# One step deeper projection pipeline, an early query projection, and ScalarE's square root in a six-layer windowed attention kernel

## The chip, the core and the metric

The kernel runs on one core of a Trainium2 chip. The metric is the device time of one execution in microseconds; several executions are timed, and one more is profiled.

## What is computed

The input is one sequence of 2048 tokens with 128 channels. First comes a recurrent mixing layer (RWKV-like) with its normalisation, which the change does not touch. Then come six layers, each of windowed attention and a gated feed-forward block, and a last normalisation. Per layer, cut to what matters here:

```
x = attn(shift_tokens(x)) + x          # half of the channels are taken from the token before
x = ffn(shift_tokens(x)) + x
attn:  q, k, v = split(x @ Wqkv)       # 16 heads of 64
       q = l2norm(q) * q_scale         # t / max(norm(t), 1e-12)
       k = l2norm(k) * k_scale
       q = q*cos*scale + rotate_half(q)*sin*scale;   k likewise with 1/scale
       window of 32: each query sees its own block and the block before it
       softmax(8 * q @ k.T + mask) @ v, then @ Wo
ffn:   layernorm -> @ W1 + b1 -> a * gelu(gate) -> @ W2 + b2
```

## The kernel before

The program is written by hand in raw instructions: each engine has its own queue of instructions, and semaphores with counts order them (`after(engine, semaphore, n)` waits for a count of n, and for nothing where n is not positive). Tokens are cut into 16 tiles of 128 (`TILES`), so six layers have 96 tile steps, numbered through the layers (`STEPS`, `tile_of`, `layer_of`). Activations lie channel by token in `xa` (before attention) and `xb` (after it).

`layers()` is a software pipeline. Each engine's `step(s, h, odd, live)` does, for step s, the parts of several tiles in one fixed order:

- **p = s+1**, projection: TensorE projects q (L1278) into `proj_a`, k (L1293) into `proj_b`, and later v (L1350) into `proj_a`. ScalarE squares q and k (L1054), VectorE sums the squares per head (L1155), takes the inverse root of the sums by nine small operations (`inverse_root`, L88 to L104: a guess from the exponent's bits, two polishing steps), and scales q and k to `unit` (L1180). The rotation is `across` (GpSimd, L999), `along` (GpSimd for q at L1032, VectorE for k at L1233) and their sum `rotated` (GpSimd, L1006). ScalarE copies v to `val` (`v_tok`, L1114).
- **a = s**, scores: TensorE transposes q and k (L1246, to `turn`), ScalarE copies them out (L1083, L1089), TensorE adds the mask (L1332) and makes the scores (L1338), VectorE takes the row maxima and subtracts them (L1169, L1172), ScalarE takes the exponential (L1061).
- **b = s-1**, output: TensorE transposes the probabilities (L1246), ScalarE copies them (L1074), TensorE mixes the values (L1312, semaphore `mixed`), VectorE divides by the mass (L1161), TensorE transposes the heads (L1246) and multiplies by Wo (L1379), VectorE adds to `xb` (L1223).
- Every second step has one part of the feed-forward block of a pair of tiles. **Odd** steps have `down`: Gelu on ScalarE (L1068), the gating on VectorE (L1196, semaphore `gated`), W2 on TensorE (L1357), the sum into `xa` (L1219); and the deviations of the next pair (L1363, L1131, L1132). **Even** steps have `up`: the normalised tile is transposed (L1372), scaled (L1122), and multiplied by W1 at the end of TensorE's step (`widen`, L1262).

TensorE's order in a step is: transposes of the probabilities (b), query projection (p), key projection (p), transposes of q (a), the mix (b), transposes of k (a), transposes of the heads (b), mask and scores (a), value projection (p), down and deviations or the normalised tile's transposes, Wo (b), and in even steps the wide projection. The key projection waits in odd steps for `gated` (L1285), since the wide projection's output leaves the same bank. The query projection waits for `v_laid` of the tile before (L1275), that is for ScalarE's copy of v out of the bank.

**The values' way.** The mix needs v by windows of 64 keys (the own block of 32 and the one before) on the right partitions. So after each copy of v, SyncE issues 16 transfers of 64 KB from `val` to `v_win` (`spread`, L933 to L948). `val` and `v_win` have two buffers each. The counts that order this are:

```
spread(m):   wait v_laid >= m + 1;  wait mixed >= 2 * (m - 1)     # L936, L938; mixed counts 2 per tile
             16 transfers, each adds 16 to v_spread               # 256 per spread
ScalarE's copy of v of tile p:   wait v_projected >= 2 * p + 2;  wait v_spread >= 256 * p     # L1112, L1113
TensorE's mix of tile b:         wait v_spread >= 256 * b + 256                               # L1306
```

SyncE's queue also holds the weight loads of the next layer, each behind the last use of the old ones, between the spreads.

The steps before s = 7 and the last ones are written out (`run`, L919), the 88 between them are a loop of 44 rounds of an odd and an even step on every engine.

Of the kernel before, what the change touches and what calls it, by code (L numbers as in the profile page):

```python
# [25 lines left out]
I32 = mybir.dt.int32  # L26
# [36 lines left out]
ROOT_SCALE = 3 / 8  # L63
# [15 lines left out]
ROOT_OPS = 9  # L79


def inverse_root(dve, ops, x, bound, y, work, magic, done, before):

    for i in ops:
        if i:
            dve.wait_ge(done, before + i)
        if i == 0:
            op = dve.scalar_tensor_tensor(bound, x, 1e-24, x, ALU.max, ALU.max)  # L88
        elif i == 1:
            op = dve.scalar_tensor_tensor(y.bitcast(I32), bound.bitcast(I32), -0.5, magic.bitcast(I32), ALU.mult, ALU.add)  # L90
        elif i == 2:
            op = dve.tensor_tensor(work[0], y, y, ALU.mult)
        elif i == 3:
            op = dve.tensor_tensor(work[1], work[0], bound, ALU.mult)
        elif i == 4:
            op = dve.scalar_tensor_tensor(work[0], work[1], -10.0 / 3.0, work[1], ALU.add, ALU.mult)
        elif i == 5:
            op = dve.scalar_tensor_tensor(y, work[0], 5.0, y, ALU.add, ALU.mult)
        elif i == 6:
            op = dve.scalar_tensor_tensor(work[0], y, -0.5 * ROOT_SCALE ** 2, y, ALU.mult, ALU.mult)  # L100
        elif i == 7:
            op = dve.tensor_tensor(work[1], work[0], bound, ALU.mult)
        else:
            op = dve.scalar_tensor_tensor(y, work[1], 1.5, y, ALU.add, ALU.mult)  # L104
        op.then_inc(done, 1)
# [711 lines left out]
def layers(nc, ctx, given):  # L817
# [12 lines left out]
    with ExitStack() as own:  # L830
# [8 lines left out]
        magic = sb("magic", [128, 2, HEADS])  # L839
# [4 lines left out]
        sums_min = sb("sums_min", [128, 2, HEADS])  # L844
# [5 lines left out]
        rotated = [sb(f"rotated{i}", [128, HEADS, HEAD]) for i in range(2)]  # L850
# [21 lines left out]
        warm = sb("warm", [128, 1])  # L872

        warmed = sem("warmed")
# [7 lines left out]
        rooted = sem("rooted")  # L882
# [19 lines left out]
        FIRST, ROUNDS = 7, 44  # L902
# [27 lines left out]
        with nc.Block() as block:  # L930
            @block.sync
            def _(sp):
# [23 lines left out]
                for m in range(5):  # L956
                    spread(m, m % 2)
                with sp.Fori(0, 5) as i:
                    spread(i * 2 + 5, 1)
                    spread(i * 2 + 6, 0)  # L960
                with sp.Fori(1, DEPTH) as layer:
# [12 lines left out]
                    load_when(load_down, xa_ready, layer * (TILES // 2) + XA_BASE, layer)  # L974
                    with sp.Fori(0, 5) as i:
                        spread(first + i * 2 + 5, 1)
                        spread(first + i * 2 + 6, 0)
                spread(STEPS - 1, 1)

            @block.gpsimd  # L980
            def _(pool):
# [19 lines left out]
                def add_turned(j, p):  # L1001
# [546 lines left out]
```

## Time and profile before

| | |
|---|---|
| median of 3 runs | 2007.84 us (2001.0 to 2007.87) |
| the profiled execution | 2001.63 us, span in the trace 1999.8 us |
| TensorE matmuls busy | 1771.6 us (89% of the span) |
| VectorE busy | 1543.1 us (77%) |
| GpSimd busy | 1454.8 us (73%) |
| ScalarE busy | 1156.1 us (58%) |
| granted TensorE clock, mean | 0.975 |
| first and last query projection of a step (L1278) | 194.6 and 1922.6 us |

In the rows, PE is TensorE's matmuls, PEld its weight loads, DVE VectorE, ACT ScalarE, POOL GpSimd, SP SyncE and SPq its queue. L12 is line 12 of the kernel. A helper's line stands for all its calls: L1246 is every transpose. Times are in microseconds from the start of the span, durations of one are in ns where the view says so. A matmul's end is modelled: a row's length reaches somewhat beyond the start of the next group, so distances between starts tell more. "PEclk" is the granted clock as a share of full speed.

### The profile page before, as it was taken

The numbers are of one execution on the slowest core, as the hardware profiler recorded it, in microseconds if no ns is written. First come the engines' busy times: TensorE is split into PE (matmuls) and PEld (weight loads), VectorE is DVE, ScalarE is ACT, GpSimd is POOL, SyncE is SP. The second block draws the span as 40 slices with busy tenths as digits, with TensorE's granted clock in tenths as the row PEclk, the third lists the DMA queues.
The fourth block names the chain that finished last, engine by engine and source line by source line (L and its number), as shares of the span: only waits on it lengthen the run. The fifth ranks groups of instructions, "written<-read, shape, count | busy, mean of one in ns | idle before, by whom it ended". The sixth has DMA issues, their size and how long they took to land. (4 is left out here: it accounts for less than half of the span.)

```text
span 1999.8 us, 85355 instructions
## 1 busy us (share of the span) xinstructions
PE 1771.6 (89%) x34184; PEld 1277.4 (64%) x34184; DVE 1543.1 (77%) x2729; ACT 1156.1 (58%) x1966; POOL 1454.8 (73%) x967
## 2 busy tenths in 40 slices
PE   7764789999999999999999999999999999999995
PEld 3453466666666666666666666666666666666664
DVE  4774798778878877788788777887887788778864
ACT  2311456666666666666666666666666666666663
POOL 3221787787788778877887787778777877887771
PEclk9985899999999999999999999999999999999998
DMA  4000222223232223222223322233222232322220
GB/s 151 2 3 1 56 63 57 64 60 84 66 74 58 54 55 94 63 68 58 63 56 85 76 67 55 52 81 81 62 58 62 61 86 63 74 60 52 55 63 22
DMA packets 93581, 123.43 MB, mean 62 GB/s; under 512 B 27760, under 2 KB 41808, under 8 KB 93392
## 3 DMA queue, kind: packets, MB, share of 16 engines
q1 hardware_dynamic: 93232, 122.42, 24.3%
q8 instruction: 46, 0.75, 0.2%
q10 hardware_dynamic: 288, 0.13, 0.0%
q14 instruction: 15, 0.12, 0.0%
HBM read 20.74 MB, written 1.05 MB: 11 GB/s over the span
## 5 line engine op out<-in xcount | busy, mean ns | idle before, releaser
L999 POOL TENSOR_TENSOR across<-unit,turns 128x1024 f32<-128x1024 f32 x192 | 497.4, 2591 | 275.5 <-issue 265.6
L1006 POOL TENSOR_TENSOR rotated<-along,across 128x1024 f32<-128x1024 f32 x192 | 495.7, 2582 | 14.2
L1155 DVE TENSOR_REDUCE sums<-squares 128x16 f32<-128x1024 f32 x192 | 234.0, 1219 | 177.9 <-ACT squares L1054 177.7
L1246 PE MATMUL turn<-identity,rotated 128*128 128x128 f32 x1536 | 204.7, 276 | 35.5 <-POOL rotated L1006 34.3
L1246 PEld LDWEIGHTS turn<-identity,rotated 128*128 128x128 f32 x1536 | 172.3, 141 | 98.0 <-issue 82.5
L1032 POOL TENSOR_TENSOR along<-unit,turns 128x1024 f32<-128x1024 f32 x96 | 228.0, 2375 | 0.0
L1350 PE MATMUL proj_a<-w_qkv,shift_a 128*128 128x512 f32 x384 | 189.5, 616 | 36.3 <-DVE unit L1180 30.1
L1114 ACT COPY val<-proj_a 128x1024 f32<-128x1024 f32 x96 | 97.2, 1012 | 180.7 <-PE proj_a L1350 180.7
L1379 PE MATMUL att<-o_t,w_o 128*128 128x128 f32 x1536 | 188.9, 277 | 0.0
L1278 PE MATMUL proj_a<-w_qkv,shift_a 128*128 128x512 f32 x384 | 184.4, 603 | 5.0 <-POOL shift_a L989 3.7
L1379 PEld LDWEIGHTS att<-o_t,w_o 128*128 128x128 f32 x1536 | 181.0, 193 | 1.0 <-issue 1.0
L1089 ACT COPY k_t<-turn 128x512 f32<-128x512 f32 x192 | 103.2, 589 | 134.5 <-PE turn L1246 134.5
L1293 PE MATMUL proj_b<-w_qkv,shift_a 128*128 128x512 f32 x384 | 180.9, 593 | 0.0
L1233 DVE TENSOR_TENSOR along<-unit,turns 128x1024 f32<-128x1024 f32 x96 | 165.7, 1726 | 0.0
L1054 ACT ACTIVATE squares<-proj_a 128x1024 f32<-128x1024 f32 x96 | 98.2, 1023 | 115.8 <-PE proj_a L1278 115.8
L1312 PE MATMUL att<-v_win,p_t 64*32 64x64 f32 x12288 | 154.2, 225 | 0.8 <-ACT p_t L1074 0.8
L1338 PEld LDWEIGHTS turn<-k_t,q_t 64*32 64x32 f32 x12288 | 128.3, 105 | 41.4 <-issue 41.1
L1074 ACT COPY p_t<-att 128x512 f32<-128x512 f32 x192 | 103.1, 589 | 89.0 <-PE att L1246 89.0
L1312 PEld LDWEIGHTS att<-v_win,p_t 64*32 64x32 f32 x12288 | 135.6, 105 | 20.1 <-issue 16.9
L1161 DVE TENSOR_TENSOR heads_out<-att,inv_mass 128x512 f32<-128x512 f32 x192 | 123.6, 686 | 31.4 <-PE att L1312 31.4
L1338 PE MATMUL turn<-k_t,q_t 64*32 64x64 f32 x12288 | 144.2, 225 | 0.0
L1172 DVE TENSOR_TENSOR logits<-turn,row_max 128x512 f32<-128x512 f32 x192 | 132.8, 692 | 6.7
(201 smaller groups left out, 3366.2 us busy)
## 6 DMA issues: line engine op xcount, KB each, us to landing
v_win<-val SPq DMA_DIRECT2D x1536, 64.0 KB, 2.0
w_qkv<-wqkv_dram SPq DMA_DIRECT2D x18, 512.0 KB, 3.9
w_o<-wo_dram SPq DMA_DIRECT2D x6, 512.0 KB, 4.7
where<-positions_dram SPq DMA_DIRECT2D x1, 2048.0 KB, 10.7
w_ffn<-ffn_dram SPq DMA_DIRECT2D x12, 170.5 KB, 2.3
w_ffn<-ffn_dram SPq DMA_DIRECT2D x6, 192.0 KB, 2.3
x_tok<-x_dram SPq DMA_DIRECT2D x4, 256.0 KB, 4.2
out_dram<-final SPq DMA_DIRECT2D x4, 256.0 KB, 2.4
```

Of the source, the lines that this page charges most:

```text
L999: pool.tensor_tensor(a[:, :, ::-1, :], u, table, ALU.mult).then_inc(acrossed[j], 1)
L1006: pool.tensor_tensor(rotated[j][:, :, :], along[j][:, :, :], across[j][:, :, :], ALU.add).then_inc(rotated_in[j], 1)
L1032: pool.tensor_tensor(along[0][:, :, :], unit[0][:, :, :], turns[mine][:, 0, :].unsqueeze(1).broadcast_to([128, HEADS, HEAD]), ALU.mult).th ...
L1155: dve.tensor_reduce(sums[:, j, :], squares[j][:, :, :], AX.X, ALU.add).then_inc(summed[j], 1)
L1233: dve.tensor_tensor(along[1][:, :, :], unit[1][:, :, :], turns[mine][:, 2, :].unsqueeze(1).broadcast_to([128, HEADS, HEAD]), ALU.mult).the ...
L1246: mm = pe.transpose(bank[:, TILE * (i % 4):TILE * (i % 4) + TILE], buffer[:, TILE * i:TILE * i + TILE], identity[:, :])
L1278: mm = pe.matmul(bank_a[:, half, :], shift_a[mine][:, :], w_qkv[:, 512 * half:512 * half + 512], start=True, stop=True)
L1293: mm = pe.matmul(bank_b[:, half, :], shift_a[mine][:, :], w_qkv[:, base:base + 512], start=True, stop=True)
L1312: mm = pe.matmul(bank_s[WINDOW * w:WINDOW * w + WINDOW, par, HEAD * a_:HEAD * a_ + HEAD], p_t[rows, a_, WINDOW * w:WINDOW * w + WINDOW], v ...
L1338: mm = pe.matmul(bank_t[WINDOW * w:WINDOW * w + WINDOW, par, HEAD * a_:HEAD * a_ + HEAD], q_t[rows, a_, WINDOW * w:WINDOW * w + WINDOW], k ...
L1350: pe.matmul(bank_a[:, par, :].rearrange("p (a e) -> p a e", a=PAIRS), shift_a[mine][:, :], values[:, par, :, :], start=True, stop=True).th ...
L1379: mm = pe.matmul(bank_s[:, 0, 0:TILE], w_o[:, a_, :], o_t[:, a_, :], start=(a_ == 0), stop=(a_ == PAIRS - 1))
```

## The change

- **Depth.** The projection part works on p = s+2 instead of s+1, on every engine. So `rotated` gets two buffers by the parity of the tile, and a tile's q and k are transposed two steps after their projection. The pipeline starts at s = -2; the loop has 43 rounds, and the parities of `turns`, `shift_a` and `val` are turned.
- **Early query projection.** The query projection of tile s+3 is issued at the end of step s, after Wo and before the wide projection. Its squares are the first thing in ScalarE's next step, ahead of the Gelus and the copies of the probabilities; their sum is the first thing in VectorE's, ahead of the mass.
- **Root.** ScalarE takes a Relu with bias -1e-24 and a Sqrt with bias 1e-24 of the 128x32 sums, between the copies of q and of k. VectorE takes the reciprocal and one Newton step, four operations instead of nine, behind a wait for ScalarE's root. The factor 3/8 in the position tables goes with the old root.
- **Sets of functions.** ScalarE loads the set of sqrt ahead of the k squares and the set of exp behind the carry of the keys, in each step; the warming exponential of odd steps (L1093) goes.
- **SyncE.** The order of spreads and weight loads is shifted by one spread at four places. `spread` itself, and the two waits of the copy of v, are as they were.

The diff, cut to its core (the parity renamings, `mine` to `odd` for p, are left out):

```diff
-ROOT_OPS = 9
+ROOT_OPS = 4
+TINY = 1e-24
...
+def inverse_root(dve, x, root, y, work, done, before):
+
+    dve.reciprocal(y, root).then_inc(done, 1)
+    dve.wait_ge(done, before + 1)
+    dve.scalar_tensor_tensor(work[0], y, -0.5, y, ALU.mult, ALU.mult).then_inc(done, 1)
+    dve.wait_ge(done, before + 2)
+    dve.scalar_tensor_tensor(work[1], x, TINY, work[0], ALU.max, ALU.mult).then_inc(done, 1)
+    dve.wait_ge(done, before + 3)
+    dve.scalar_tensor_tensor(y, work[1], 1.5, y, ALU.add, ALU.mult).then_inc(done, 1)
...
-        rotated = [sb(f"rotated{i}", [128, HEADS, HEAD]) for i in range(2)]
+        rotated = [[sb(f"rotated{i}_{k}", [128, HEADS, HEAD]) for i in range(2)] for k in range(2)]
...
-        FIRST, ROUNDS = 7, 44
+        FIRST, ROUNDS = 7, 43
...
-            return {"p": 0 <= s + 1 < STEPS, "a": 0 <= s < STEPS, "b": 0 <= s - 1 < STEPS, "next": 0 <= s + 2 < STEPS,
+            return {"p": 0 <= s + 2 < STEPS, "a": 0 <= s < STEPS, "b": 0 <= s - 1 < STEPS, "next": 0 <= s + 3 < STEPS,
...
-            for s in range(-1, FIRST):
+            for s in range(-2, FIRST):
...
                     load_when(load_projection, k_projected, first, layer, 1)
+                    spread(first - 2, 0)
                     load_when(load_projection, v_projected, 2 * first, layer, 2)
                     spread(first - 1, 1)
                     spread(first, 0)
+                    spread(first + 1, 1)
                     load_when(load_wo, attended, first, layer)
-                    spread(first + 1, 1)
                     spread(first + 2, 0)
+                    spread(first + 3, 1)
                     load_when(load_up, widened, layer * (NC_ * TILES // 2), layer)
-                    spread(first + 3, 1)
                     spread(first + 4, 0)
                     load_when(load_down, xa_ready, layer * (TILES // 2) + XA_BASE, layer)
...
-                    after(pool, (q_turned, k_turned)[j], 2 * p)
+                    after(pool, (q_turned, k_turned)[j], 2 * (p - 1))
...
             def _(act):
...
-                    p, a, b, mine = s + 1, s, s - 1, 1 - odd
+                    p, a, b, mine = s + 2, s, s - 1, 1 - odd
...
+                    if live["p"]:
+                        square(0)
                     if live["down"]:
...
                     if live["p"]:
-                        square(0)
+                        act.preload_act_table_set("sqrt_and_others")
                         square(1)
...
+                    if live["p"]:
+                        act.wait_ge(summed[0], p + 1)
+                        act.wait_ge(summed[1], p + 1)
+                        after(act, rooted, ROOT_OPS * p)
+                        act.activation(lifted[:, :, :], sums[:, :, :], ACT.Relu, bias=tiny[:, 0:1]).then_inc(above_tiny, 1)
+                        act.wait_ge(above_tiny, p + 1)
+                        act.activation(root[:, :, :], lifted[:, :, :], ACT.Sqrt, bias=tiny[:, 1:2]).then_inc(roots_in, 1)
...
-                    if live["down"]:
-                        after(act, warmed, h)
-                        act.activation(warm[:, :], ones[:, 0:1], ACT.Exp).then_inc(warmed, 1)
...
+                        act.preload_act_table_set("exp_and_others")
                     if live["p"]:
                         act.wait_ge(v_projected, 2 * p + 2)
                         after(act, v_spread, 256 * p)
...
             def _(dve):
...
+                    if live["p"]:
+                        sum_squares(0)
                     if live["b"]:
                         dve.wait_ge(weighed, 2 * b + 2)
...
                     if live["p"]:
-                        sum_squares(0)
                         sum_squares(1)
...
+                        dve.wait_ge(roots_in, p + 1)
+                        inverse_root(dve, sums[:, :, :], root[:, :, :], inv_norm[:, :, :],
+                                     [w[:, :, :] for w in root_work], rooted, ROOT_OPS * p)
...
             def _(pe):
...
+                def project_queries(m, parity):
+                    pe.wait_ge(shifted, 2 * m + 2)
+                    pe.wait_ge(q_in, (layer_of(m) + 1) * 16)
+                    after(pe, v_laid, m)
+                    stand_alone(pe, passed)
+                    for half in range(2):
+                        mm = pe.matmul(bank_a[:, half, :], shift_a[parity][:, :], w_qkv[:, 512 * half:512 * half + 512],
+                                       start=True, stop=True)
+                    mm.then_inc(q_projected, 1)
...
                         mm.then_inc(attended, 1)
+                    if live["next"]:
+                        project_queries(s + 3, mine)
                     if live["up"]:
                         pe.wait_ge(normed_f, h + 2)
...
+                project_queries(0, 0)
                 run(pe, step)
```

## Rows read from the trace of the kernel before

**Rows 1.** one stretch: us; busy PE, PEld, DVE, ACT, POOL, PEclk, DMA share
```profile
663.80:1027.60 363.80, 338.44 (x6597) 246.60 (x6596) 292.63 (x509) 230.22 (x389) 291.83 (x190) 1.00 0.26 65
```

**Rows 2.** the waits, waiting line, releaser: us in all, times, longest us
```profile
PE turn L1246 <- POOL rotated L1006: 34.3, 51, 1.9
```

**Rows 3.** time line of TensorE: start us, us, what, [idle before <-releaser]
```profile
1002.45 1.96 PE L1350 MATMUL proj_a<-w_qkv,shift_a 128*128 128x512 f32 x4 [0.49 <-DVE unit L1180]
...
1008.56 1.06 PE L1246 MATMUL att<-identity,probs 128*128 128x128 f32 x8 [0.62 <-issue]
1009.46 1.88 PE L1278 MATMUL proj_a<-w_qkv,shift_a 128*128 128x512 f32 x4
1011.18 1.88 PE L1293 MATMUL proj_b<-w_qkv,shift_a 128*128 128x512 f32 x4
1012.89 1.04 PE L1246 MATMUL turn<-identity,rotated 128*128 128x128 f32 x8
1013.86 1.59 PE L1312 MATMUL att<-v_win,p_t 64*32 64x64 f32 x128
...
1020.28 1.96 PE L1350 MATMUL proj_a<-w_qkv,shift_a 128*128 128x512 f32 x4 [0.23 <-DVE unit L1180]
...
1024.40 1.99 PE L1262 MATMUL proj_b<-normed,w_ffn 128*128 128x256 f32 x8 [0.16 <-ACT normed L1122]
...
1027.10 1.04 PE L1246 MATMUL att<-identity,probs 128*128 128x128 f32 x8
```

**Rows 4.** time line of SyncE's queue, the first and last of one spread's sixteen
```profile
1005.78 0.51 SPq L945 DMA_DIRECT2D v_win<-val  x1
...
1015.21 0.59 SPq L948 DMA_DIRECT2D v_win<-val  x1
```

**Rows 5.** DMA issues on the page: count, KB each, us from issue to landing
```profile
v_win<-val SPq DMA_DIRECT2D x1536, 64.0 KB, 2.0
```

**Rows 6.** time line of ScalarE around two value copies
```profile
1004.52 1.01 ACT L1114 COPY val<-proj_a 128x1024 f32<-128x1024 f32 x1 [1.99 <-PE proj_a L1350]
...
1022.35 1.01 ACT L1114 COPY val<-proj_a 128x1024 f32<-128x1024 f32 x1 [1.73 <-PE proj_a L1350]
...
1024.88 1.28 ACT L1068 ACT_TABLE_LOAD   x1
1026.18 0.84 ACT L1068 ACTIVATE gelu<-proj_b,w_ffn 128x256 f32<-128x256 f32 x2
1027.30 0.47 ACT L1068 ACTIVATE gelu<-turn,w_ffn 85x256 f32<-85x256 f32 x1 [0.28 <-PE turn L1262]
```

**Rows 7.** groups by line and form: count, busy us, mean ns, idle before
```profile
L1155 DVE TENSOR_REDUCE sums<-squares 128x16 f32<-128x1024 f32 x192 | 234.0, 1219 | 177.9 <-ACT squares L1054 177.7
...
L1054 ACT ACTIVATE squares<-proj_a 128x1024 f32<-128x1024 f32 x96 | 98.2, 1023 | 115.8 <-PE proj_a L1278 115.8
...
L104 DVE SCALAR_TENSOR_TENSOR inv_norm<-root_work,inv_norm 128x32 f32<-128x32 f32 x96 | 18.4, 192 | 3.3
```

**Rows 8.** time line of VectorE, from the mass to the last gating
```profile
1026.00 1.21 DVE L1187 TENSOR_REDUCE mass<-probs 128x16 f32<-128x1024 f32 x1
...
1028.25 0.47 DVE L1196 SCALAR_TENSOR_TENSOR hidden<-turn,w_ffn,gelu 85x256 f32<-85x256 f32 x1
```

**Rows 9.** time line of TensorE, near the start and in the last steps
```profile
227.43 1.06 PE L1246 MATMUL att<-identity,probs 128*128 128x128 f32 x8 [2.53 <-ACT probs L1061]
...
1945.44 1.55 PE L1246 MATMUL turn<-identity,rotated 128*128 128x128 f32 x8 [1.95 <-POOL rotated L1006]
1946.78 1.91 PE L1246 MATMUL att<-identity,heads_out 128*128 128x128 f32 x8
1948.49 1.02 PE L1332 MATMUL turn<-band_bf,identity_bf 128*128 128x512 bf16 x2
```

**Rows 10.** time line of TensorE, the first two query projections
```profile
194.66 3.75 PE L1278 MATMUL proj_a<-w_qkv,shift_a 128*128 128x512 f32 x4 [3.68 <-POOL shift_a L989]
...
210.97 3.75 PE L1278 MATMUL proj_a<-w_qkv,shift_a 128*128 128x512 f32 x4 [1.30 <-ACT val L1114]
```

More of the change, by code:

```diff
@@ L955, in _ @@
                 sp.wait_ge(cleared, 2)
-                for m in range(5):
+                for m in range(6):
                     spread(m, m % 2)
-                with sp.Fori(0, 5) as i:
-                    spread(i * 2 + 5, 1)
+                with sp.Fori(0, 4) as i:
                     spread(i * 2 + 6, 0)
+                    spread(i * 2 + 7, 1)
                 with sp.Fori(1, DEPTH) as layer:
@@ L1011, in step @@
                 def step(s, h, odd, live):
-                    p, mine = s + 1, 1 - odd
+                    p = s + 2
                     if live["p"]:
@@ L1016, in step @@
                         after(pool, alonged[0], p - 1)
-                        pool.tensor_tensor(turns[mine][:, :, :], where[:, tile_of(p), :, :], scales[:, layer_of(p), :, :],
+                        pool.tensor_tensor(turns[odd][:, :, :], where[:, tile_of(p), :, :], scales[:, layer_of(p), :, :],
                                            ALU.mult).then_inc(table_made, 1)
@@ L1113, in step @@
                         after(act, v_spread, 256 * p)
-                        act.copy(v_tok[mine][:, :, :, :], bank_a[:, :, :].rearrange("p a (h e) -> p a h e", e=HEAD))\
+                        act.copy(v_tok[odd][:, :, :, :], bank_a[:, :, :].rearrange("p a (h e) -> p a h e", e=HEAD))\
                             .then_inc(v_laid, 1)
@@ L1149, in step @@
                 def step(s, h, odd, live):
-                    p, a, b, mine = s + 1, s, s - 1, 1 - odd
+                    p, a, b, mine = s + 2, s, s - 1, 1 - odd
                     def sum_squares(j):
@@ L1233, in step @@
                         dve.tensor_tensor(along[1][:, :, :], unit[1][:, :, :],
-                                          turns[mine][:, 2, :].unsqueeze(1).broadcast_to([128, HEADS, HEAD]),
+                                          turns[odd][:, 2, :].unsqueeze(1).broadcast_to([128, HEADS, HEAD]),
                                           ALU.mult).then_inc(alonged[1], 1)
@@ L1272, in step @@
                     if live["p"]:
+                        pe.wait_ge(k_in, (layer_of(p) + 1) * 16)
                         pe.wait_ge(shifted, 2 * p + 2)
-                        pe.wait_ge(q_in, (layer_of(p) + 1) * 16)
-                        after(pe, v_laid, p)
-                        stand_alone(pe, passed)
-                        for half in range(2):
-                            mm = pe.matmul(bank_a[:, half, :], shift_a[mine][:, :], w_qkv[:, 512 * half:512 * half + 512],
-                                           start=True, stop=True)
-                        mm.then_inc(q_projected, 1)
-                    if live["p"]:
-                        pe.wait_ge(k_in, (layer_of(p) + 1) * 16)
                         after(pe, united[1], p)
@@ L1292, in step @@
                             base = INNER + 512 * half
-                            mm = pe.matmul(bank_b[:, half, :], shift_a[mine][:, :], w_qkv[:, base:base + 512],
+                            mm = pe.matmul(bank_b[:, half, :], shift_a[odd][:, :], w_qkv[:, base:base + 512],
                                            start=True, stop=True)
@@ L1320, in step @@
                             pe.wait_ge(q_laid, 2 * a + j + 1)
[L1321 removed]
+                            transposes(bank_t[:, j, :], rotated_flat[odd][1], j, k_turned)
                     if live["b"]:
```

80 lines of the change are left out of this document (28 added, 52 removed).

## The prediction

> **What bounds the kernel now.** I read the busy time by stretch first, then the waits, and then one pair of steps in the order of time, because the change is made inside a loop whose body is such a pair. In the middle of the layers TensorE is busy 338 of 364 us, no other engine over 293, at a granted clock of 1.00, the full one of its two levels (2.4 GHz) [rows 1]. The first and the last query projection are 1728 us apart (194.6 to 1922.6) for 95 steps, 18.19 us a step, so that the stretch of 363.8 us is ten pairs of steps and a pair takes **36.38 us**. So TensorE's own work is nearly the bound, and what a better order can win is its waits. Two of them are what the deeper pipeline is aimed at: the transposes of q and k wait 34.3 us in all for GpSimd's sum [rows 2], and the value projection waits 0.49 and 0.23 us in a pair for the normalised heads [rows 3]. The time line shows two more, 0.62 us before the transposes of the probabilities after an odd step and 0.16 us before the wide projection [rows 3]. Together some 2 us of a pair: if all went and nothing came, 46.5 pairs would give 93 us back.
>
> I call a step odd where s is odd (it has the Gelu, the gating and the down projection) and even where the wide projection ends it. M is the end of a step's `mixed` matmuls (L1312).
>
> **The wait that decides.** The change leaves three conditions as they are and moves the work around them. ScalarE's copy of the values (L1114) waits for `v_spread` of 256*p, that is for all spreads up to p-1; with p = s+2 these are the spreads up to s+1, where before they were those up to s. SyncE's spread of m waits for the mix of m-2 (L938), so spread s+1 waits for the mix of s-1, and that is the one made **in the same step s**. Before, the spread that the copy needs began right after the copy of the step before (the row of SyncE at 1005.78 stands 0.25 us behind the end of the copy that starts at 1004.52) and issued its last transfer at 1015.21, 2.0 us before it landed [rows 4 to 6]: 1017.2, while the next copy started at 1022.35. It had 5.1 us to spare. Now it can't start before M = 1015.45 (1013.86 + 1.59 [rows 3]), so the spread would land at 1027.1 and the copy is 4.8 us late, 6.5 once the query projection no longer stands ahead of the value projection. Behind the copy on ScalarE's queue stand both exponentials and the normed copy; on TensorE the early query projection waits for `v_laid`, and everything of the next step stands behind it. That closes a ring from mix to mix.
>
> **The ring, piece by piece.** From M to the spread's first issue I take 0.25 us, the distance just read; fifteen distances of 0.629 us (1005.78 to 1015.21) are 9.43, the landing 2.0 [rows 4, 5]: 11.7. What a DMA's landing takes to release ScalarE no row shows; between 0 and the 0.25 of the other wake-ups I take 0.1. The copy therefore starts at M + 11.8. It lasts 1.01 [rows 6], TensorE wakes 0.25 later and the query projection takes 1.72 from start to start of the next (1009.46 to 1011.18) [rows 3]: the next group starts 2.98 us after the copy's start. The exponential and the normed copy that the wide projection needs are through by then (in the trace of before a Gelu load can start 2.53 us after the copy's start, with both exponentials done [rows 6]).
> - From an odd step into an even one there follow the transposes of the probabilities (0.90), the key projection (1.71), the transposes of q (0.97) and the mix (1.59) [rows 3]. Sum: 11.8 + 2.98 + 5.17 = **19.95 us**.
> - From an even step into an odd one the wide projection comes first (2.70), the probabilities' transposes end at 2.98 + 2.70 + 0.90 = 6.58 after the copy's start, and there the key projection waits for `gated`, because the gated values leave its bank. Before, the query projection stood between and covered this. The new order also puts the squares and the sum of q ahead of it: queries are ready at 1.26 + 1.88 = 3.14, the squares take 1.02, the set load for Gelu 1.28, three Gelus 1.6 with a wait inside, 1.3 without it (1026.18 to 1027.77) [rows 3, 6, 7], to about 6.9. On VectorE the sum of the q squares (1.22) runs from 4.3 to 5.5, and mass, reciprocal and three gatings take 2.72 (1026.00 to 1028.72) [rows 8]: 8.25. The key projection starts at 8.5, 1.9 late, the mix ends 4.27 later: 12.77. Sum: 11.8 + 12.77 = **24.55 us**.
>
> The pair takes 44.5 us instead of 36.38, so 8.1 more. The ring turns in steps 1 to 93, 46.5 pairs: **+377 us**.
>
> **The other parts.** *Root.* Nine small operations of VectorE become four behind two of ScalarE; five fewer at 0.19 us [rows 7] are some 1 us less on VectorE's queue, and a longer chain through a second engine; from the sum of the k squares to the value projection there are several us in the new schedule (TensorE has no work left from about M + 9 or 11 to M + 13), so I price both at nothing. If the ring were not there, this would be worth the 0.3 us a step that the value projection waits now [rows 3]. *Set loads.* The load of the exp set that the warming operation brings once in a pair goes and four come, five loads in a pair instead of two, 3.84 us of ScalarE at 1.28 each. The sqrt load stands ahead of the k squares, which come behind M; the exp load stands where ScalarE then waits for the spread. Priced at nothing, covered by the ring's 11.8; without the ring the sqrt load would delay the q copies by about 1 us a step. A Gelu starts 0.02 us after its load's end [rows 6], so a load costs its own row. The Trainium skill ("ScalarE: Activation LUTs", What ACT_TABLE_LOAD costs) counts a drain of about 1380 ns on top of the load's own 1283 at each switch to another set. By that rule the Gelus of each pair would come 1.38 us later behind the new squares, and the estimate from the page would be up to 64 us more than mine; no trace of before shows such a drain.
> *Early query projection.* The same four matmuls, elsewhere; counted in the ring. *GpSimd.* Its sum has a whole further step before it is read, so the 34.3 us of [rows 2] go, into a ring that is longer anyway. *SyncE.* The weight loads stay between the same spreads or move by one; a spread's transfers may queue behind one projection's load once or twice in each of five layers. Nothing to a few us each; I take nothing.
> *Start and end.* There is one more step that only projects: 16.3 us (194.66 to 210.97) [rows 10]. One full step of 18.2 goes and one without projections comes, 18.2 less three projections of about 1.8, 12.9. Net +11, I take **+10 us**.
>
> **The clock.** In the new schedule TensorE idles before each query projection: from the value projection (M + 7) the rest of an even step is about 2.3 us of work, an odd one's 3.7 (1020.28 to 1024.40, and 1002.45 to 0.62 before 1008.56, each less 1.8 for the value projection itself) [rows 3], so 3.9 us of idleness in an even step and some 2 in an odd one, and 1.9 more at the key projection. After an idle time of 1.95 us in the last steps two groups of eight transposes took 1.55 and 1.91 us instead of 1.04 [rows 3, 9], and the band's matmuls behind them 1.02: the clock was at its lower level (1.2 GHz), which cost 1.4 us in these two groups and, as I estimate, 1.7 with the band's. After 2.53 us near the start it did not fall (1.06) [rows 9]. So between nothing and both rings paying 1.7 to 2 (4 us a pair). I take one spell of 1.7 in each pair, since the one after 3.9 us is near certain but half absorbed by the 1.9 us that TensorE waits for `gated`, and the other comes about half of the time: **+79 us**.
>
> **Sum.** The profiled execution took 2001.63 us (span 1999.8), 0.3% under the median of the three runs, 2007.84, and near their lowest. 2001.6 + 377 + 79 + 10 = **2468 us**, 23% above it.
>
> **Rivals.**
> 1. *The copy does not wait, and the pipeline does what it is for.* It decides where the spread lasts less than the way from the mix to the end of the value projection, 1020.28 + 1.96 - 1015.45 = 6.8 us [rows 3], or where I misread the counts. Then a pair loses the 2.0 us of waits and gets the `gated` wait of 1.9, or not: 2001.6 + 10 and between 0 and -93, 1920 to 2010, middle 1960. For it: the waits of [rows 2] are real. Against it: sixteen issues at 0.629 us, and nothing in the change shortens them. 7 in 100, of which 4 below 1998.
> 2. *The clock falls in both rings of each pair and stays down longer* (6 us after short gaps that follow each other): 5 us a pair instead of 1.7, 2001.6 + 377 + 10 + 233 = 2620. For it: gaps in every step. Against it: 75% of busy time. 10 in 100.
> 3. *The ring holds, but the clock does not fall and the key projection does not wait*: 42.6 a pair, 2001.6 + 289 + 10 = 2300. 8 in 100.
> 4. *Slower by another wait alone*, the `gated` chain with the k squares behind the sqrt load, with no spread on the ring: 1.9 + 1 less the 2.0, 2001.6 + 42 + 10 = 2054. 3 in 100.
>
> **How the numbers follow.** The forecast has the remaining 72 in 100. Its own bounds: without a fall of the clock 2389, with 4 us a pair 2575; 0.1 us more or less at the landing moves it by 9. From 2340 to 2590 lie the forecast and the nearer halves of rivals 2 and 3; rivals 1 and 4 and the farther halves, 19 in 100, are left outside. 0.5% (10 us) is about what a measurement of this kernel can tell from no change. Faster than that: 4 in 100 (most of rival 1); within it: 2; slower: 94.
>
> **What would show it.** In the profile after: in each step the first transfer to v_win starts about 0.25 us behind the end of the mix instead of behind the value copy; ScalarE's idle time before the value copy grows from 1.7 us [rows 6] to more than 4, and ends with the transfers; the query projection starts 0.25 us after each copy; odd and even steps of 20 and 24.5 us; an idle 1.9 us before the key projection in odd steps; TensorE's busy share near 76% (36.4 less 2.0 of waits, in 44.5) and a clock below 1.00 in the middle stretches. The q transposes no longer wait for GpSimd. The prediction is wrong if the value copy follows its projection by less than 2 us, or if the spread's transfers come quicker when they start later; its size is wrong if a pair without falls of the clock is not near 44.5 us.

## The result, and the profile after

The changed kernel takes **2480.7 us** (median of 4 runs, 2474.4 to 2486.5) against 2005.7 us for the kernel before in the same rounds: ratio 1.237, 95% interval 1.233 to 1.241. The forecast was 2468 us. The profiled execution took 2482.8 us (span 2481.0).

The page, first part and clock; busy us (share) of each engine:

```profile
PE 1940.1 (78%) x34184; PEld 1354.8 (55%) x34184; DVE 1493.3 (60%) x2250; ACT 1373.1 (55%) x2253; POOL 1449.1 (58%) x965
...
PEclk9967888899999999999999999999999999999998
...
L1109 ACT COPY val<-proj_a 128x1024 f32<-128x1024 f32 x96 | 97.2, 1012 | 484.1 <-DMA v_win<-val 471.0
```

The stretch of [rows 1], now (us; busy PE, PEld, DVE, ACT, POOL; PEclk, DMA share, GB/s):

```profile
663.80:1027.60 363.80, 292.23 (x5167) 206.41 (x5155) 223.57 (x325) 216.36 (x355) 228.87 (x150) 0.94 0.22 53
```

The waits (total, times, longest):

```profile
ACT val L1109 <- DMA v_win<-val: 471.0, 93, 7.7
PE proj_a L1259 <- issue: 277.7, 86, 5.0
...
PE proj_b L1293 <- DVE hidden L1194: 62.9, 45, 1.8
```

Every engine is busy for a smaller share of the stretch than in [rows 1], so no engine became the bound: something makes them all wait. The waits name it. ScalarE's copy of the values waits for the spread's transfers 93 times, 5.1 us each. TensorE's query projection waits for that copy: the view puts 9 of its waits (37.3 us) down to it and 86 to "issue", but in the turn below the projections at 1210.36, 1231.55 and 1256.88 each start 0.10 us behind the end of a copy. The wait of [rows 2], for GpSimd's sum, has gone.

One turn of the ring. TensorE, from before a query projection in an odd step to the one after the next step:

```profile
1205.83 1.95 PE L1379 MATMUL att<-o_t,w_o 128*128 128x128 f32 x16
1210.36 2.44 PE L1259 MATMUL proj_a<-w_qkv,shift_a 128*128 128x512 f32 x4 [2.58 <-issue]
1212.60 1.91 PE L1244 MATMUL att<-identity,probs 128*128 128x128 f32 x8
1214.31 2.28 PE L1293 MATMUL proj_b<-w_qkv,shift_a 128*128 128x512 f32 x4
1216.42 1.04 PE L1244 MATMUL turn<-identity,rotated 128*128 128x128 f32 x8
1217.39 1.48 PE L1312 MATMUL att<-v_win,p_t 64*32 64x64 f32 x128
...
1223.50 1.95 PE L1350 MATMUL proj_a<-w_qkv,shift_a 128*128 128x512 f32 x4
...
1231.55 3.15 PE L1259 MATMUL proj_a<-w_qkv,shift_a 128*128 128x512 f32 x4 [4.09 <-issue]
1234.49 2.44 PE L1270 MATMUL proj_b<-normed,w_ffn 128*128 128x256 f32 x8
...
1239.97 1.95 PE L1293 MATMUL proj_b<-w_qkv,shift_a 128*128 128x512 f32 x4 [1.31 <-DVE hidden L1194]
...
1242.73 1.48 PE L1312 MATMUL att<-v_win,p_t 64*32 64x64 f32 x128
...
1256.88 1.96 PE L1259 MATMUL proj_a<-w_qkv,shift_a 128*128 128x512 f32 x4 [2.56 <-issue]
```

The granted clock in short stretches of the same turn (columns as above): the gap before the first query projection, the projection, the mix; then the second gap, projection and widening; then the third gap and projection:

```profile
1207.80:1210.30 2.50, 0.00 (x0) 0.00 (x0) 0.29 (x1) 1.05 (x2) 2.50 (x2) 1.00 0.22 52
1210.40:1212.50 2.10, 2.10 (x4) 0.83 (x5) 0.88 (x2) 1.45 (x4) 0.71 (x2) 0.81 0.00 0
...
1217.40:1218.80 1.40, 1.40 (x129) 1.31 (x128) 1.12 (x1) 1.22 (x3) 0.22 (x1) 1.00 0.00 0
...
1227.50:1231.50 4.00, 0.00 (x0) 0.00 (x0) 3.01 (x2) 1.06 (x2) 4.00 (x2) 1.00 0.27 66
1231.60:1234.40 2.80, 2.80 (x4) 1.11 (x5) 0.00 (x0) 1.35 (x3) 2.67 (x2) 0.60 0.00 0
1234.60:1236.70 2.10, 2.10 (x9) 1.79 (x8) 0.72 (x1) 1.87 (x2) 1.64 (x3) 0.77 0.00 0
...
1254.40:1256.80 2.40, 0.00 (x0) 0.00 (x0) 0.29 (x1) 1.03 (x2) 2.40 (x2) 1.00 0.21 51
1256.90:1258.60 1.70, 1.70 (x4) 0.77 (x5) 0.46 (x2) 1.47 (x4) 0.42 (x1) 1.00 0.00 0
```

A mean between 0.5 and 1 is a stretch that lies partly at 1.2 and partly at 2.4 GHz. The matmuls behind the first two gaps pay, those behind the third do not. In other pairs the clock falls while TensorE still waits; a projection and a stretch of the gap before it:

```profile
1137.59 3.75 PE L1259 MATMUL proj_a<-w_qkv,shift_a 128*128 128x512 f32 x4 [3.46 <-issue]
```

```profile
1136.70:1137.50 0.80, 0.00 (x0) 0.00 (x0) 0.65 (x1) 0.80 (x2) 0.80 (x1) 0.50 0.00 0
```

Counted over the 77 query projections from 612.0 to 2360.6 us: behind the 39 short gaps (2.56 to 2.69 us, after an odd step) the clock fell 19 times and stayed at 1.00 in 20; behind the 38 long ones (3.46 to 4.17 us) it fell each time, in 22 of them before TensorE had resumed.

SyncE's queue in the same turn, first and last of the sixteen:

```profile
1219.00 0.51 SPq L928 DMA_DIRECT2D v_win<-val  x1
...
1228.44 0.59 SPq L931 DMA_DIRECT2D v_win<-val  x1
```

ScalarE:

```profile
1224.08 1.28 ACT L1105 ACT_TABLE_LOAD   x1
1230.44 1.01 ACT L1109 COPY val<-proj_a 128x1024 f32<-128x1024 f32 x1 [5.08 <-DMA v_win<-val]
...
1235.85 1.28 ACT L1058 ACT_TABLE_LOAD   x1
1237.15 0.84 ACT L1058 ACTIVATE gelu<-proj_b,w_ffn 128x256 f32<-128x256 f32 x2
```

Read across the three: the mix ends at 1218.87 (1217.39 + 1.48), the first transfer goes out at 1219.00, the last at 1228.44, and 2.00 us later the copy starts. The values it copies were ready at about 1225.3. The query projection follows 1.11 us behind the copy's start, and from it everything up to the next mix.

A **pair of steps** is the measure for all that follows. It is the time from the first weight load of the first query projection to the last weight load of the last one, over 47.5 pairs (95 steps): 36.38 us before, (2383.1 - 200.4) / 47.5 = **45.95 us** after. (The table of before calls 1922.6 the last query projection; its matmuls start at 1921.7, and after they start at 2381.9. From starts alone both pairs are 0.02 us shorter.) The difference, 9.57, makes 455 of the 481 us between the two profiled executions; the other 26 lie at the start and the end. The turn shown above, with a fall behind both gaps, took 46.52 us, the figure that some of the expectations use.

### The profile page after: what moved, and what is told of

The parts are those of the page before. It is cut to its first block and busy times, and to the rows that moved or that the text cites. A ratio compares the mean times of both kernels' runs of the same rounds, so it can differ in the third digit from the quotient of the medians.

```text
span 2481.0 us, 85249 instructions
## 1 busy us (share of the span) xinstructions
PE 1940.1 (78%) x34184; PEld 1354.8 (55%) x34184; DVE 1493.3 (60%) x2250; ACT 1373.1 (55%) x2253; POOL 1449.1 (58%) x965
## 5 line engine op out<-in xcount | busy, mean ns | idle before, releaser
L1259 PE MATMUL proj_a<-w_qkv,shift_a 128*128 128x512 f32 x384 | 289.6, 898 | 318.6 <-issue 277.7
L992 POOL TENSOR_TENSOR rotated<-along,across 128x1024 f32<-128x1024 f32 x192 | 452.4, 2356 | 17.8 <-POOL along L1018 7.0
L1259 PEld LDWEIGHTS proj_a<-w_qkv,shift_a 128*128 128x128 f32 x384 | 89.4, 256 | 412.0 <-issue 412.0
L1293 PE MATMUL proj_b<-w_qkv,shift_a 128*128 128x512 f32 x384 | 190.5, 619 | 62.9 <-DVE hidden L1194 62.9
L1350 PE MATMUL proj_a<-w_qkv,shift_a 128*128 128x512 f32 x384 | 191.0, 620 | 15.3 <-issue 14.2
L1231 DVE TENSOR_TENSOR along<-unit,turns 128x1024 f32<-128x1024 f32 x96 | 196.6, 2048 | 0.1
L1338 PEld LDWEIGHTS turn<-k_t,q_t 64*32 64x32 f32 x12288 | 143.5, 105 | 49.2 <-issue 41.2
L1338 PE MATMUL turn<-k_t,q_t 64*32 64x64 f32 x12288 | 167.1, 225 | 0.4 <-issue 0.4
L1312 PE MATMUL att<-v_win,p_t 64*32 64x64 f32 x12288 | 143.6, 226 | 2.4 <-issue 1.4
L1244 PE MATMUL att<-identity,heads_out 128*128 128x128 f32 x768 | 104.8, 279 | 47.8 <-DVE heads_out L1157 47.8
L1293 PEld LDWEIGHTS proj_b<-w_qkv,shift_a 128*128 128x128 f32 x384 | 69.9, 203 | 124.3 <-issue 124.3
```

The source lines that it names most:

```text
L992: pool.tensor_tensor(rotated[odd][j][:, :, :], along[j][:, :, :], across[j][:, :, :], ALU.add).then_inc(rotated_in[j], 1)
L1231: dve.tensor_tensor(along[1][:, :, :], unit[1][:, :, :], turns[odd][:, 2, :].unsqueeze(1).broadcast_to([128, HEADS, HEAD]), ALU.mult).then ...
L1244: mm = pe.transpose(bank[:, TILE * (i % 4):TILE * (i % 4) + TILE], buffer[:, TILE * i:TILE * i + TILE], identity[:, :])
L1259: mm = pe.matmul(bank_a[:, half, :], shift_a[parity][:, :], w_qkv[:, 512 * half:512 * half + 512], start=True, stop=True)
L1293: mm = pe.matmul(bank_b[:, half, :], shift_a[odd][:, :], w_qkv[:, base:base + 512], start=True, stop=True)
L1312: mm = pe.matmul(bank_s[WINDOW * w:WINDOW * w + WINDOW, par, HEAD * a_:HEAD * a_ + HEAD], p_t[rows, a_, WINDOW * w:WINDOW * w + WINDOW], v ...
```

## The experiments

The theory: a ring from mix to mix through the spread sets the pair, the clock's falls add some us to it, and the gated wait adds its part. The rivals: another wait does it, or the root, or the order of the squares.

**1. Is it the ring?** The transfers of a spread that read the value buffer of the tile before go first and count apart. The other fourteen follow. The copy then waits for the two of its predecessor's spread, and otherwise only for the spread before that.

```diff
+                    after(sp, v_carried, 32 * m)
+                    stand_alone(sp, passed)
+                    for par in range(2):
+                        last = old[TILE - WINDOW:TILE, par, :, :].rearrange("p a e -> p (a e)")
+                        sp.dma_start(v_win[odd][2 * WINDOW * par:2 * WINDOW * par + WINDOW, 0, :], last).then_inc(v_carried, 16)
+                    after(sp, v_spread, 224 * m)
...
-                        after(act, v_spread, 256 * p)
+                        after(act, v_carried, 32 * p)
+                        after(act, v_spread, 224 * (p - 1))
...
-                        pe.wait_ge(v_spread, 256 * b + 256)
+                        pe.wait_ge(v_carried, 32 * b + 32)
+                        pe.wait_ge(v_spread, 224 * b + 224)
```

> The changed kernel, with the two transfers of a spread that read the older value buffer issued first and counted by a semaphore of their own; ScalarE's value copy waits for these two alone (and for the spread before), so it needs 0.25 + 0.63 + 2.0 = about 2.9 us from the mix instead of 11.6, less than the 6.8 us to the end of the value projection. Theory (the ring mix - spread - value copy - query projection sets the pace): the ring is gone, TensorE's own work and the wait for the gated values remain, 34.4 to 36.4 us a pair instead of 46.5, so 1920 to 2010 us, the clock near 1.00. Rival (set loads, ScalarE's root or the squares ahead of the Gelus are what slows it): above 2300 us.

Measured: 2061.5 us, ratio 1.028 (1.024 to 1.033); 37.17 us a pair. SyncE in this kernel, the first transfers of the spread and the last ones:

```profile
1204.25 1.16 SPq L927 DMA_DIRECT2D v_win<-val  x2
1205.59 1.14 SPq L935 DMA_DIRECT2D v_win<-val  x2
...
1213.75 0.59 SPq L938 DMA_DIRECT2D v_win<-val  x1
```

ScalarE, and TensorE's key projection in the next odd step:

```profile
1211.16 1.01 ACT L1118 COPY val<-proj_a 128x1024 f32<-128x1024 f32 x1
```

```profile
1220.35 1.95 PE L1302 MATMUL proj_b<-w_qkv,shift_a 128*128 128x512 f32 x4 [2.19 <-DVE hidden L1203]
```

The copy starts while the same spread is still being issued (1211.16 against 1213.75), and 419 of the 475 us go. **The ring is shown.** The expectation of 1920 to 2010 was missed by 50 us: the deeper pipeline without its ring is still slower than the kernel before. TensorE's longest waits there are the key projection's for the gated values, 95.3 us over 45 steps (experiment 6 takes it up), and 56.5 us for the heads before their transposes (24.9 before; not tried apart). Some 20 us more lie at the start and the end.

**2. The same ring in the kernel before.** Only the spread's wait is tightened, so that there too it starts behind the mix of the same step.

```diff
-                    after(sp, mixed, 2 * (m - 1))
+                    after(sp, mixed, 2 * m)
```

> The kernel before, with one number changed: the spread of tile m waits for the mix of m-1 instead of m-2, which is what the deeper pipeline does to it. Nothing else of the change. Theory: the same ring. From an odd step into an even one 11.6 + 2.5 (copy, two exponentials) + 6.9 (transposes, both projections, transposes, mix) = 21.0; from an even one into an odd 11.6 + 2.05 + 2.70 + 6.9 = 23.3; 44.3 us a pair, 2372 us, and up to 2485 with the falls of the clock that the changed kernel has (2.4 us a pair). Middle 2430. Rival (the other parts of the change make it slow): near 2005 us.

Measured: 2549.7 us, ratio 1.274 (1.268 to 1.279); 47.7 us a pair at a mean clock of 0.88. Its waits:

```profile
ACT val L1114 <- DMA v_win<-val: 610.5, 94, 8.7
PE proj_b L1262 <- ACT normed L1122: 238.3, 47, 7.1
PE att L1246 <- ACT probs L1061: 191.9, 49, 6.8
```

One number in a wait gives the kernel before the same loss, and more. No new operation is needed for it. The size lies 65 us above the top of the expectation (2485). TensorE's gaps are longer here (5.03 and 3.65 us a pair) and its granted clock in the stretch of [rows 1] is lower (0.89 against 0.94), which fits, but in this kernel the clock was not tried apart.

**3. A shorter spread.** Twelve of the sixteen transfers are made; the windows of the fourth block are left out, and the mix reads zeros there. The other waits count 192.

```diff
-                        for w in range(BLOCKS):
+                        for w in range(BLOCKS - 1):
```

> The changed kernel with twelve of the sixteen transfers of each spread: the fourth block's windows are left out, so the mix reads zeros there. Theory: the ring is shorter by four issues of 0.63 us in every step, 5.0 us a pair, 237 us in all: 2244 us; with the falls of the clock gone as well, since the idle gaps before the query projection shrink to 1.6 and 0.1 us, down to 2130. Rival (the spread is not on the path): 2480 us.

Measured: 2136.1 us, ratio 1.067 (1.062 to 1.072); 38.73 us a pair. The wait of the copy:

```profile
ACT val L1109 <- DMA v_win<-val: 217.1, 93, 4.6
```

Four issues of 0.63 us less, twice a pair, are 5.0 us; the pair lost 7.2. The other 2.2 fit what the falls of the clock cost (next experiment); in this kernel it was granted 1.00 in the stretch of [rows 1].

**4. The clock.** TensorE is kept busy in the gap before the early query projection by added matmuls whose result nobody reads, 5 in odd and 9 in even steps, in a second version 2 and 4.

```diff
+                    if live["next"] and live["b"] and live["a"]:
+                        filler = scales[:, 0:2, :, :].rearrange("p l f e -> p (l f e)")
+                        for _ in range(5 if odd else 9):
+                            pe.matmul(bank_s[:, 1, :] if odd else bank_b[:, 0, :], identity[:, :], filler,
+                                      start=True, stop=True)
                     if live["next"]:
                         project_queries(s + 3, mine)
```

> The changed kernel with idle work for TensorE ahead of the early query projection: 5 matmuls of 128x512 at the end of an odd step, 9 at the end of an even one (2.2 and 3.9 us at the full clock, the gaps are 2.6 and 4.1), into banks that nothing reads then. Theory (the lower clock costs 2.4 us of the 46.5 of a pair): the clock stays near 1.00 and the time falls by about 110 us to 2370 (2350 to 2400). Rival (the falls are absorbed in waits): 2480 us or, where the filler reaches past the copy, more.

Measured: 2601.3 us, ratio 1.299. One such matmul of 128x512 fp32 is two in the trace and takes 0.86 us, twice what was assumed, so the filler outlasted the gap:

```profile
1210.16 7.89 PE L1385 MATMUL proj_b<-scales,identity 128*128 128x512 f32 x18
1217.89 1.88 PE L1259 MATMUL proj_a<-w_qkv,shift_a 128*128 128x512 f32 x4
```

It says nothing about the clock. With 2 and 4:

> As the run with filled gaps, but with 2 and 4 matmuls of 128x512 instead of 5 and 9: the trace of that run shows 0.86 us for each, so these are 1.7 and 3.4 us in gaps of 2.6 and 4.1. Theory (the falls of the clock lie on the ring and cost 1.5 to 2.4 us of a pair): granted clock near 1.00 and 70 to 115 us less than the changed kernel, 2365 to 2410 us. Rival (they are absorbed in waits): 2480 us.

Measured: 2372.7 us, ratio 1.183 (1.180 to 1.185). TensorE, one pair:

```profile
1207.43 1.48 PE L1312 MATMUL att<-v_win,p_t 64*32 64x64 f32 x128
...
1217.95 3.60 PE L1385 MATMUL proj_b<-scales,identity 128*128 128x512 f32 x8
1221.58 1.95 PE L1259 MATMUL proj_a<-w_qkv,shift_a 128*128 128x512 f32 x4
...
1228.81 1.96 PE L1293 MATMUL proj_b<-w_qkv,shift_a 128*128 128x512 f32 x4 [1.82 <-DVE hidden L1194]
...
1231.57 1.48 PE L1312 MATMUL att<-v_win,p_t 64*32 64x64 f32 x128
...
1245.76 1.96 PE L1259 MATMUL proj_a<-w_qkv,shift_a 128*128 128x512 f32 x4 [0.87 <-issue]
...
1251.11 1.48 PE L1312 MATMUL att<-v_win,p_t 64*32 64x64 f32 x128
```

More work for TensorE, 108 us less time. The projections keep 1.95 us where they took 2.44, 2.28 and 3.15 in the kernel after, and the pair is 43.70 us. That is the ring without the clock; the clock's part is 45.95 - 43.70 = **2.25 us a pair**. The filled kernel was granted 1.00 in the stretch of [rows 1], the kernel after 0.94.

The trace of the kernel after gives the same by itself, since half of its short gaps have no fall. Over the 77 projections counted above, the way from the projection behind a short gap to the one behind the long gap takes 19.52 us where the clock stays at 1.00 and 21.21 where it falls; in the filled kernel it takes 19.52. So the filler on that way costs nothing, and such a fall costs 1.69 us. The way from the projection behind the long gap to the next takes 25.70 us on average, with a fall each time, and 24.16 in the filled kernel.

**5. The order of the squares.** In odd steps the squares and the sum of q go behind the Gelus and the gating, as before; the ring stays.

```diff
-                    if live["p"]:
+                    if live["p"] and not live["down"]:
                         square(0)
                     if live["down"]:
...
+                    if live["p"] and live["down"]:
+                        square(0)
```

(the same for `sum_squares(0)` on VectorE)

> The changed kernel with the squares of q and their sum back behind the Gelus and the gating in odd steps (they stay first in even ones). Theory (the wait of the key projection for the gated values, 1.3 to 1.9 us in odd steps, lies on the ring because these two stand ahead of the Gelus): 60 to 90 us less, 2390 to 2420. Rival (the wait is absorbed by the spread that follows): 2480 us.

Measured: 2430.0 us, ratio 1.212 (1.209 to 1.214). The key projection's wait falls from 62.9 to 14.2 us in all, and the kernel gains 51, somewhat less than the 60 to 90 expected.

**6. Both.** Experiments 1 and 5 together.

> Carry transfers first, as in the first run, and the squares of q behind the Gelus in odd steps. Theory: the ring is gone and the wait of 2.2 us for the gated values too (37.2 us a pair less about 1.7): 1970 to 1990 us, faster than before. Rival (the wait moves on: q squares, sqrt load and k squares one after the other delay the sums of k and the copies of q): 2040 to 2060 us.

Measured: **1989.2 us** (6 runs), ratio 0.991 (0.990 to 0.993): with the ring gone and the key projection's wait down from 95.3 to 45.3 us, the deep pipeline beats the kernel before, by 0.9%. What TensorE still waits for:

```profile
PE att L1257 <- DVE heads_out L1168: 57.2, 95, 1.4
...
PE proj_b L1306 <- DVE hidden L1205: 45.3, 45, 1.1
```

**7. The root.** Experiment 6 with the root of before: nine operations on VectorE, none on ScalarE, no loads of the sqrt and exp sets, the warming exponential back.

```diff
-ROOT_OPS = 4
+ROOT_OPS = 9
...
-                        act.preload_act_table_set("sqrt_and_others")
...
-                        act.activation(root[:, :, :], lifted[:, :, :], ACT.Sqrt, bias=tiny[:, 1:2]).then_inc(roots_in, 1)
...
-                        act.preload_act_table_set("exp_and_others")
```

> The run before this one with the old inverse root: nine small operations of VectorE, no operation and no set load of ScalarE for it. Theory (ScalarE's root and its two set loads in each step cost what they save, since the sqrt load holds up the k squares by 1.3 us and with them the division and the transposes of the heads, 0.3 to 0.8 us a step): the same or up to 25 us less than the run before. Rival (the root is worth its five operations of VectorE): 15 to 30 us more.

Measured: **1985.6 us** (1984.1 to 1991.0), ratio 0.990 (0.988 to 0.991), the lowest median of all; its interval overlaps that of experiment 6. The new root moves waits about and no gain from it shows:

```profile
PE proj_a L1372 <- DVE unit L1196: 60.0, 94, 5.8
...
PE att L1265 <- DVE heads_out L1177: 34.1, 96, 1.4
```

The value projection waits some 0.7 to 0.9 and 0.25 us in a pair for the longer chain on VectorE, a wait that experiment 6 does not have, but the heads come earlier and the gated values too (14.2 us in all instead of 45.3).

**8. The root on the ring.** The same exchange in the changed kernel itself.

> The changed kernel with the old inverse root: nine small operations of VectorE, no operation and no set load of ScalarE for it; depth and early query projection stay. Theory (the root and its set loads stand beside the ring): the same time as the changed kernel within 15 us, 2465 to 2495. Rival (ScalarE's root and four set loads in a pair, 3.8 us, are part of what was lost): 2300 to 2400 us.

Measured: 2477.9 us, ratio 1.237 (1.233 to 1.240); the kernel after has 2480.7. On the ring the root is worth nothing either way.

**9. The early query projection without the depth.** The kernel before, with the query projection of tile s+2 behind Wo, nothing else (43 rounds of the loop instead of 44, the rest written out).

```diff
                     if live["p"]:
+                        pe.wait_ge(k_in, (layer_of(p) + 1) * 16)
                         pe.wait_ge(shifted, 2 * p + 2)
-                        pe.wait_ge(q_in, (layer_of(p) + 1) * 16)
-                        after(pe, v_laid, p)
...
+                    if live["next"]:
+                        project_queries(s + 2, odd)
                     if live["up"]:
```

> The kernel before with the early query projection alone: that of tile s+2 behind Wo in step s. Depth, root and the order of ScalarE and VectorE stay. The spread that the value copy needs is then the one of the step before, so there is no ring. Theory: the 0.62 and 0.16 us that TensorE waits before the probabilities' transposes and the wide projection go, the waits for GpSimd's sum (0.6 us a pair) stay, some 0.3 us for the gated values come: 0.5 us a pair, about 1980 us (1970 to 1995). Rival (the depth is what brings the gain of the last two runs): 2000 us or more.

Measured: 1996.4 us (10 runs), ratio 0.996 (0.994 to 0.997), less than half the gain expected. The wait of [rows 2] doubled:

```profile
PE turn L1246 <- POOL rotated L1006: 69.3, 52, 3.6
```

That fits a TensorE that reaches the transposes earlier, while GpSimd's sum comes no earlier. In experiment 7, where the depth gives the sum a further step before it is read, TensorE has no such wait, and the ratio is 0.990.

**10. The squares of q earlier.** Experiment 9 with the squares and the sum of q first in even steps.

> The run before this one with the squares of q and their sum first in even steps on ScalarE and VectorE, as in the change. Theory (the division of the heads and the normalised heads come earlier where the sums are out of the way): up to 15 us less than the run before, 1965 to 1985. Rival (in even steps neither waits for them): the same as the run before.

Measured: 1997.5 us, ratio 0.996 (0.994 to 0.997), the same as experiment 9. An earlier start of q does not help, so the lateness lies behind it, in GpSimd's queue or at k; which of the two was not tried.

## Why the prediction was right, step by step

**The wait that decides: right.** The copy waits 93 times, as many as the steps 1 to 93 that were named. It is the first experiment that shows it is this wait, since the view of waits alone can't tell a cause from a follower.

**The ring's pieces: right, the wake-ups a little too long.** From the end of the mix to the first issue it is 0.13 us, where 0.25 was taken; the landing releases ScalarE with nothing on top of the 2.00 us, where 0.1 was added; TensorE follows the copy's end by 0.10, not 0.25. From M, the end of a mix, to the query projection it is 12.67 and 12.71 us (experiment 4) instead of 13.06. The rest of the way was 11.47 and 6.83 us instead of 11.51 and 6.9. The gated wait, worked out as 1.9 us, was 1.82 at the full clock. Step by step it is 19.52 and 24.16 us at the full clock instead of 19.95 and 24.55, and over all pairs 43.70 us a pair instead of 44.5. The ring's term comes to 7.32 x 47.5 = 348 us, **29 us less than the 377 on record**: the shorter pair takes 36 off, and counting it over all 47.5 pairs instead of 46.5 puts 7 back. The mis-sized term is the wake-up of 0.25: it was read from one place in the trace of before, SyncE behind ScalarE's copy, and used for the hand-overs between other engines.

**The clock: right in kind, too small.** 2.25 us a pair instead of 1.7, over 47.5 pairs 107 us instead of 79, **28 more**. The forecast took 1.7 us for each fall, half of the short gaps with one, and the long gap's fall half absorbed by the gated wait: 0.85 and 0.85. The short gaps came out so: 19 of 39 with a fall, 1.69 us each, 0.82 a pair. (The forecast called such a gap "some 2 us", but its own terms give 13.06 - 6.8 - 3.7 = 2.6, and 2.58 was measured.) The long gap is what was mis-sized: 25.70 - 24.16 = 1.54 us instead of 0.85. The fall itself has about the size assumed. Behind the 4.09 us gap the query projection took 2.94 us to the next start instead of 1.79, and the first part of the wide projection 2.27 instead of 1.73, together 1.69. But the gated wait swallows little of it: it is 62.9 us over 45 steps against 81.2 in the filled kernel, so 0.41 us a pair is absorbed, not half of 1.7.

**Start and end: 26 us instead of 10, 16 more.** The first query projection stands at 200.4 instead of 194.6, of which part is run to run (194.8 to 202.5 in the other kernels). From the last weight load of the last one to the end it is 97.9 us instead of 77.2. The forecast counted the extra step at the speed of the loop before; in fact TensorE waits 4.52 us there for the probabilities, and matmuls behind it run at the lower clock (eight transposes take 1.91 us instead of 1.04, the mix 1.93 instead of 1.48; granted clock 0.50 from 2410 to 2413). How the rest of the 20.7 us divides was not worked out.

Together: 2001.6 + 348 + 107 + 26 = 2482.6, the profiled execution's 2482.8. The three errors, -29, +28 and +16, left 15 us: the forecast was nearer than its terms, and that is luck.

**Priced at nothing.** *Root and set loads* (experiment 8): right, 2.8 us within the scatter. The ring is the cover, as said, and the rows show the load of exp in the time in which ScalarE waits. In this trace too the Gelu starts 0.02 us behind the end of the load at 1235.85, so a load costs its own row. The Trainium skill ("ScalarE: Activation LUTs", What ACT_TABLE_LOAD costs) adds a drain of about 1380 ns to each switch of sets; the trace does not agree. *Without the ring* the forecast said that the sqrt load would delay the q copies by about 1 us a step, and that the root would be worth the value projection's wait. Experiments 6 and 7 show the second (a wait of 60.0 us with the old root, none with the new). Against it the new root has 23 us more of waiting for the heads and 31 for the gated values, 54 us or 0.6 a step; that the sqrt load is behind these was not tried apart. The two sides cancel (3.6 us in favour of the old root, with intervals that overlap). *GpSimd*: right, its wait has gone from the list. Experiment 9 shows what it is with the early query projection and without the depth: 69.3 us.

**The rivals.** The first, that the copy does not wait, is false. The second, a clock that falls in both rings of each pair and costs 5 us, is false here: it fell behind each long gap but behind half of the short ones, for 2.25 us. The third, neither clock nor gated wait, is false; both are there. The fourth, the gated wait alone, is false for this kernel but comes near the one of experiment 1: it gave 2054 us, and 2061.5 was measured, with the wait for the heads beside the gated one.

## What to carry to other kernels

Before moving a producer one step further ahead, write down each wait as "step n of this needs step m of that" and shift the indices: a count that is not touched in the diff can turn from a wait on the step before into a wait on the same step, and then a double buffer closes a ring. The length of that ring is a plain sum of durations from the old trace and can be worked out beforehand. When such a change fails, look for the smallest part of the resource that makes the ring; here it was two of sixteen transfers, and letting them go first turned 2480.7 us into 2061.5.

## What the runs showed of the hardware

- Sixteen SBUF to SBUF transfers of 64 KB are issued 0.63 us apart on one queue, and a waiting ScalarE starts 2.00 us after the last issue; 2.0 us is also the median from issue to landing in the trace of before [rows 5].
- A matmul of 128x512 in fp32 is two in the trace, 0.86 us together at the full clock; the filler of experiment 4 was sized at half of it.
- Behind idle gaps of TensorE of 2.56 to 2.69 us the granted clock fell in 19 of 39 cases, and behind gaps of 3.46 to 4.17 us in 38 of 38. The length of a short gap does not tell the two kinds apart: there were gaps of 2.57 us with a fall and of 2.69 us without. The fall began up to 1.0 us before TensorE resumed (22 cases) or up to 1.4 us after.
- A fall behind a short gap cost 1.69 us of the step. Filling the gaps with unused work made the kernel 108 us faster.
